# First stage of a four-stage block: channels on the partitions from the scan to the output projection

## What is computed

```python
def _mamba_block(x, in_proj_w, conv_w, conv_b, dt_bias, A_log, D, norm_w, out_proj_w, ln_w, ln_b):
    zxbcdt = jnp.einsum('bld,ed->ble', x, in_proj_w)
    z = zxbcdt[..., :D_INNER]
    ...
    def step(h, inp):
        dA_t, x_t, B_t, C_t, dt_t = inp
        dBx = dt_t[:, :, None, None] * x_t[..., None] * B_t[:, None, None, :]
        h = h * dA_t[:, :, None, None] + dBx
        y = jnp.einsum('bhpn,bn->bhp', h, C_t)
        return (h, y)
    ...
    y = ys.transpose(1, 0, 2, 3) + D[None, None, :, None] * x_ssm
    y = y.reshape(b, l, D_INNER)
    y = y * jax.nn.silu(z)
    y = y * lax.rsqrt(jnp.mean(y * y, axis=-1, keepdims=True) + EPS) * norm_w
    y = jnp.einsum('bld,ed->ble', y, out_proj_w) + x
    mu = jnp.mean(y, axis=-1, keepdims=True)
    var = jnp.mean((y - mu) ** 2, axis=-1, keepdims=True)
    return (y - mu) * lax.rsqrt(var + EPS) * ln_w + ln_b
```

## Time and profile before

| | |
|---|---|
| median of 3 runs | 1599.17 us (1599.06 to 1600.42) |
| profiled execution | 1601.12 us, span of its instructions 1599.2 us |
| TensorE busy | 1442.7 us, 90% of the span |
| VectorE busy | 1209.4 us, 76% |
| ScalarE busy | 820.1 us, 51% |
| GpSimd busy | 796.9 us, 50% |
| granted TensorE clock | 0.969 of full speed, on average |
| first three layers | to about 1080 us |
| last layer | from there to the end |

### The profile page before, as it was taken

One profiled execution on the slowest core, in us unless ns is written; L12 is line 12 of the kernel. 1 busy time (PEld: TensorE's weight loads), 2 busy tenths in 40 slices (PEclk: granted clock), 3 DMA queues, 4 the chain that ended last, 5 costly groups with the idle time before them and its releaser, 6 DMA issues. The chain is left out here.

```text
span 1599.2 us, 32323 instructions
## 1 busy us (share of the span) xinstructions
PE 1442.7 (90%) x10752; PEld 1262.2 (79%) x10752; DVE 1209.4 (76%) x2290; ACT 820.1 (51%) x1846; POOL 796.9 (50%) x2004
## 2 busy tenths in 40 slices
PE   5588999999999999999999999754999999869997
PEld 4366788788888788887888877543999999869997
DVE  4466798898898898898898887533888888827664
ACT  2234544544544545545445443202676777557775
POOL 0332253563563463463563552233777777657763
PEclk9997999999999999999999999866999999989999
DMA  6000000000000000000000000006677766867782
GB/s 233 7 7 1 8 1 14 15 1 14 15 1 14 14 2 14 15 1 14 15 1 14 8 5 5 7 7 207 177 197 197 191 184 191 265 245 302 302 323 70
DMA packets 140752, 132.10 MB, mean 83 GB/s; under 512 B 7376, under 2 KB 130512, under 8 KB 134096
## 3 DMA queue, kind: packets, MB, share of 16 engines
q1 hardware_dynamic: 140624, 130.50, 25.9%
HBM read 73.85 MB, written 56.62 MB: 82 GB/s over the span
## 5 line engine op out<-in xcount | busy, mean ns | idle before, releaser
L622 PE MATMUL bk<-ve_f,oe 128*128 128x128 f32 x2048 | 277.0, 279 | 2.6 <-DVE ve_f L1300 2.6
L622 PEld LDWEIGHTS bk<-ve_f,oe 128*128 128x128 f32 x2048 | 249.7, 192 | 25.9 <-issue 20.7
L1300 DVE SCALAR_TENSOR_TENSOR ve_f<-ps_m,oT 128x512 f32<-128x512 f32 x256 | 171.8, 679 | 5.2 <-PE bk L622 3.4
L2187 POOL TENSOR_TENSOR d_s<-d_ex 128x1024 f32<-128x1024 f32 x32 | 131.8, 4120 | 87.1 <-ACT d_ex L1987 87.1
L1261 DVE COPY_PREDICATED vals<-oh,bk 128x1024 f32<-128x1024 int32 x112 | 146.6, 1309 | 10.6 <-PE bk L393 8.8
L1937 PE MATMUL d_sl<-d_ex,e_prT 128*128 128x128 f32 x1024 | 135.8, 276 | 9.4 <-POOL d_ex L2204 9.4
L1871 PE MATMUL d_lg<-d_phf,d_xtf 128*128 (+1 forms) x1024 | 125.0, 282 | 15.9 <-DMA d_xtf<-x_T 6.8
L1871 PEld LDWEIGHTS d_lg<-d_phf,d_xtf 128*128 128x128 f32 x1024 | 122.0, 199 | 16.8 <-issue 7.1
L1937 PEld LDWEIGHTS d_sl<-d_ex,e_prT 128*128 128x128 f32 x1024 | 125.2, 193 | 9.7 <-POOL d_ex L2204 9.7
L1881 PE MATMUL d_sl<-d_ex,d_xs 128*128 128x128 f32 x1024 | 121.4, 277 | 5.7 <-DVE d_ex L2102 5.7
L1881 PEld LDWEIGHTS d_sl<-d_ex,d_xs 128*128 128x128 f32 x1024 | 118.5, 194 | 6.1 <-DVE d_ex L2102 6.1
(11 more groups left out here) (283 smaller groups left out, 3733.4 us busy)
## 6 DMA issues: line engine op xcount, KB each, us to landing
logits<-d_raw SPq DMA_DIRECT2D x128, 256.0 KB, 3.3
e_lt<-logits SPq DMA_DIRECT2D x32, 1024.0 KB, 5.6
y_slots<-d_ys SPq DMA_DIRECT2D x64, 256.0 KB, 4.3
d_ex<-y_slots SPq DMA_DIRECT2D x16, 1024.0 KB, 7.3
d_w<-W SPq DMA_DIRECT2D x16, 256.0 KB, 3.4
oe<-xT SPq DMA_DIRECT2D x1, 2048.0 KB, 7.8
xt_in<-xT SPq DMA_DIRECT2D x16, 128.0 KB, 2.3
x_in<-x SPq DMA_DIRECT2D x16, 128.0 KB, 2.4
```

The source lines that it names most:

```text
L622: last = pe.matmul(ps_u[:, cols], oe[:, hp, e, :], mo[:, n % MO, hp, :], start=False, stop=(e == NE - 1 and hp == HP - 1), skip_group_chec ...
L1300: V.scalar_tensor_tensor(mo[:, n % MO, :, :].rearrange("p a n -> p (a n)"), ps_m[:], float(NE - e), oT[:, u, c, :, :].rearrange("p a n -> ...
L2187: G.tensor_tensor(s8[:], part[:, 0:8, :], part[:, 8:16, :], ALU.add).then_inc(n, 1)
```

## The change

From the scan to the output projection, all tiles of stage a now have channels on the partitions.

- `a_z` swaps its operands: `sz` and `tz` are 2 groups of channels x 256 tokens.
- VectorE's `a_xd` makes only `xd`.
- The running sum leaves `a_bg`. In `a_state` it is now made per channel and token: four products, two for each group of channels, each with a column of `a_all` repeated 64 times as weights and `upp_s` streamed. `ep` is 128x256, made by ScalarE after it has copied `st`.
- `a_inter` is two products of 128 columns instead of one of 256.
- VectorE's `a_int` is a product with `ep` into the right half of `inter`, and two operations that add D times `xbc` (two groups).
- `a_y` swaps its operands: 64 columns of `xd` are the weights and the 128 columns of `mx` are streamed; the two heads of a group end in the two halves of the partitions.
- ScalarE squares `yg` in one operation without accumulator. The sums are made on TensorE, in a new step `a_ssq` between `b_values(6)` and the next sequence's `a_xbc`: four products with 128 columns of `sq` as weights and one column of ones. ScalarE copies the two columns to `ssq`, between `c_gelu` and `a_cin`.
- The transposes `a_yt` and the copy to `yT` are gone. `a_op` reads `yg` and stands where `a_yt` stood.
- `a_xt` stays. Temporaries of the preparation now share the place of `lx`, and two constants are filled before the first slot.

```diff
@@ TensorE @@
             def a_bg(b):
 
-                wait(pe, q["a_xd"], 2 * b + 2)
+                wait(pe, q["a_xd"], b + 1)
                 pe.transpose(ps_a[:, 0:P], xbc[:, 2, 0:P], id_f[:])
...
-                pe.matmul(ps_a[:, 3 * P:3 * P + NH], upp_s[:], a_all[:, b * C + 1, :], start=True, stop=True,
-                          skip_group_check=True).then_inc(q["a_bg_ps"], 1)
...
             def a_state(b):
                 wait(pe, q["a_gm"], b + 1)
-                wait(pe, q["a_ep"], b + 1)
                 wait(pe, q["a_btok"], b + 1)
                 wait(pe, q["a_xst"], b + 1)
                 pe.matmul(ps_a[:, 0:DI], btok[:], xst[:].rearrange("p h d -> p (h d)"),
-                          start=True, stop=True, skip_group_check=True).then_inc(q["a_st_ps"], 1)
+                          start=True, stop=True, skip_group_check=True)
+                for j in range(2):
+                    for a in range(2):
+                        half = slice(64 * a, 64 * a + 64)
+                        head = 2 * j + a
+                        last = pe.matmul(ps_a[half, DI + j * P:DI + (j + 1) * P],
+                                         a_all[:, b * C + 1, head:head + 1].to_broadcast([P, HD]), upp_s[:],
+                                         start=True, stop=True, skip_group_check=True)
+                last.then_inc(q["a_st_ps"], 1)
...
             def a_y(b):
                 wait(pe, q["a_mx"], C * b + C)
-                wait(pe, q["a_int"], 2 * b + 1)
+                wait(pe, q["a_int"], 3 * b + 1)
+                for j in range(2):
+                    for c in range(C):
+                        for a in range(2):
+                            half = slice(64 * a, 64 * a + 64)
+                            last = pe.matmul(ps_a[half, j * L + c * P:j * L + (c + 1) * P], xd[:, c, 2 * j + a, :],
+                                             mx[:, c, 2 * j + a, :], start=True, stop=True, skip_group_check=True)
+                last.then_inc(q["a_y_ps"], 1)
+
+            def a_ssq(b):
+
+                wait(pe, q["a_sq"], b + 1)
+                wait(pe, q["b_eg"], b)
+                wait(pe, q["b_x2t"], b - 2)
                 for c in range(C):
-                    for h in range(NH):
-                        last = pe.matmul(ps_a[:, c * DI + h * HD:c * DI + (h + 1) * HD], mx[:, c, h, :],
-                                         xd[:, c, h, :], start=True, stop=True, skip_group_check=True)
-                last.then_inc(q["a_y_ps"], 1)
-
-            def a_yt(b, more):
+                    for j in range(2):
+                        last = pe.matmul(ps_o[:, c:c + 1], sq[:, j, c * P:(c + 1) * P], ones[:],
+                                         start=(j == 0), stop=(j == 1), skip_group_check=True)
+                last.then_inc(q["a_ssq_ps"], 1)
+
+            def a_op(b, more):
                 wait(pe, q["a_yg"], b + 1)
                 if more:
                     wait(pe, q["a_cin"], 2 * b + 4)
...
@@ ScalarE @@
             def a_sq(b):
 
                 wait(act, q["a_yg"], b + 1)
-                for c in range(C):
-                    if c == 1:
-                        wait(act, q["a_sq"], C * b + 1)
-                    nc.scalar.activation(sq[:], yg[:, c, :], ACT.Square, scale=0.5, accum_out=ssq[:, c:c + 1]
-                                         ).then_inc(q["a_sq"], 1)
-
-            def a_yt(b):
-                wait(act, q["a_yt_ps"], b + 1)
-                wait(act, q["a_op_ps"], b)
-                copy(yT[:].rearrange("p j n -> p (j n)"), ps_a[:]).then_inc(q["a_yt"], 1)
+                wait(act, q["a_ssq_ps"], b)
+                nc.scalar.activation(sq[:], yg[:], ACT.Square, scale=0.5).then_inc(q["a_sq"], 1)
+
+            def a_ssq(b):
+                wait(act, q["a_ssq_ps"], b + 1)
+                wait(act, norms["rms"]["rstd"], RSQRT_OPS * b)
+                copy(ssq[:], ps_o[:, 0:C]).then_inc(q["a_ssq"], 1)
@@ VectorE @@
                 V.tensor_tensor(xd[:], ps, dt_all[:, b * C:(b + 1) * C, :].unsqueeze(3).to_broadcast([P, C, NH, HD]), ALU.mult
                                 ).then_inc(q["a_xd"], 1)
-                V.tensor_tensor(xD[:], ps, d_h[:].unsqueeze(1).unsqueeze(3).to_broadcast([P, C, NH, HD]), ALU.mult
-                                ).then_inc(q["a_xd"], 1)
...
-                V.tensor_tensor(inter[:], ps_a[:, DI:2 * DI].rearrange("p (h d) -> p h d", h=NH),
-                                ep[:].unsqueeze(2).to_broadcast([P, NH, HD]), ALU.mult).then_inc(q["a_int"], 1)
-                wait(dve, q["a_int"], 2 * b + 1)
-                V.tensor_tensor(xD[:, 1, :, :], xD[:, 1, :, :], inter[:], ALU.add).then_inc(q["a_int"], 1)
+                V.tensor_tensor(inter[:, :, P:L], ps_a[:, 0:DI].rearrange("p (j t) -> p j t", j=2), ep[:], ALU.mult
+                                ).then_inc(q["a_int"], 1)
+                wait(dve, q["a_int"], 3 * b + 1)
+                for j in range(2):
+                    V.scalar_tensor_tensor(xD[:, j, :], xbc[:, j, :], d_h[:, j:j + 1], inter[:, j, :], ALU.mult, ALU.add
+                                           ).then_inc(q["a_int"], 1)
```

More of the change, by code:

```diff
@@ L272, in token_blocks @@
         names = """a_xbc_ps a_cin a_conv a_th a_xbc a_z_ps a_tz a_sz a_am a_seg_ps a_lx a_mx a_xt_ps a_xd
-            a_bg_ps a_btok a_ep a_gm a_xst a_st_ps a_st a_int_ps a_int a_y_ps a_y a_yg a_sq a_yt_ps a_yt
+            a_bg_ps a_btok a_ep a_gm a_xst a_st_ps a_st a_int_ps a_int a_y_ps a_y a_yg a_sq a_ssq_ps a_ssq
             a_op_ps a_r a_xb a_n a_x1t_ps a_x1h a_x1l a_x1
@@ L472, in a_yt @@
                     wait(pe, q["a_cin"], 2 * b + 4)
[L473 to L480 removed]
                 for c in range(C):
                     for j in range(2):
[L483 removed]
+                        last = pe.matmul(ps_a[:, c * D:(c + 1) * D], yg[:, j, c * P:(c + 1) * P], out_w[:, j, :],
                                          start=(j == 0), stop=(j == 1), skip_group_check=True)
@@ L534, in b_oht @@
                 wait(pe, q["b_x2t"], b - 1)
+                wait(pe, q["a_ssq"], min(b + 2, NB))
                 pe.transpose(ps_o[:, P:2 * P], oh[:].rearrange("p c h e -> p (c h e)"), id_f[:]
@@ L747, in slot @@
                     b_values(t - 1, 1 - u, 6)
+                if a:
+                    a_ssq(t)
                 if more:
@@ L764, in slot @@
                 if a:
-                    a_yt(t, more)
+                    a_op(t, more)
                 if b:
@@ L773, in slot @@
                     c_kv(t - 3)
-                if a:
-                    a_op(t)
                 if b:
@@ L910, in a_btok @@
                 copy(btok[:], ps_a[:, 0:P]).then_inc(q["a_btok"], 1)
-                wait(act, q["a_int"], 2 * b)
-                nc.scalar.activation(ep[:], ps_a[:, 3 * P:3 * P + NH], ACT.Exp).then_inc(q["a_ep"], 1)
             def a_st(b):
```

87 lines of the change are left out of this document (41 added, 46 removed).

## The result

| | before | after |
|---|---|---|
| median of 12 runs each, side by side | 1600.82 us | 1605.83 us |
| lowest, highest | 1598.27, 1602.51 | 1602.30, 1611.04 |
| profiled execution, its span | 1601.12, 1599.2 | 1611.04, 1609.1 |
| median length of a full slot | 59.04 us | 59.37 us |

What follows compares the result with a forecast made beforehand. A slot was bound by a TensorE stretch to the last value product, then VectorE and ScalarE to `rgS`. Added 0.9 us less 0.75 slack gave 0.15 us in 14 slots: 1599.17 + 2.1 = 1601.3 us, range 1595.5 to 1609.

Steps and rivals of the forecast that it cites:

- main case: Whole kernel: a full slot grows by 0 to 0.3 us, giving 1599 to 1604 us; chance 0.45.
- VectorE is late at the squares: Rival at `a_ssq`: `yg` slips a further 0.4 us, TensorE waits, the period grows 0.55, 1607 us; chance 0.25.
- TensorE ahead of the last value product: Step summing TensorE's changes in `a_bg`, `a_state`, `a_inter`, `a_y` and `a_ssq`: +0.9 us a slot.
- sign (1): Expected in TensorE's profile: `a_y` 1.1 us to the next line, the four `a_state` products 0.7, `a_ssq` 0.9.
- VectorE: Step on VectorE's work: dropping the product with D gains nothing, `a_int` +0.2 us, squares ready within 0.1 us of `a_ssq`.
- `ra` 0.15 us later: VectorE reaches `ra` at 642.08 - 0.75 + 0.9 = 642.23, so `ra` starts 0.15 us later than before.
- eats the slack first: Work added to TensorE ahead of 633.22 first uses 0.75 us of slack at `ra`, then is paid in full.
- `c_out` also moves by some 0.15. From there the slot is as before: TensorE's `c_out` waits for `kv`, ending at 642.31, and moves by some 0.15 us; nothing behind it changes further.
- One-column products: Rival at `a_ssq`: a one-column pass costs much less than 0.11 us, giving 1595 us; chance 0.17.
- The halves side by side: Passes into two halves overlap in `a_y` and `a_state`; the rival, no overlap, gave 1612 us, chance 0.07.
- The last layer and the first slots: Last layer takes what it took; effects in the first two slots about cancel, leaving 14 slots that grow.
- six signs: `a_y`, `a_state`, `a_ssq` times; `kv` wait replaces `kr`; no projection wait; longer value-product wait; `rgS` wait stays; slots 59.2 us.

Runs made afterwards that it cites:

- e3: Kernel before plus four unread one-column products on TensorE behind value product 6, where `a_ssq` stands in the changed kernel: ratio 1.0077, slots of 59.97 us.
- e10: Changed kernel with `a_op` back behind `c_kv` and a 128x512 ScalarE copy where the one to `yT` was: ratio 1.0100, slots of 60.07 us.
- e8: Changed kernel with TensorE's second turning of probabilities (three transposes) moved ahead of `c_out`: ratio 1.0022 to the kernel before, slots of 59.18 us.
- e2: Changed kernel with the sums of squares in one pass each instead of two, from squares rounded to F32R: ratio 1.0008, slots of 59.00 us.
- e4: Kernel before plus four unread one-column products on TensorE ahead of `b_rgb(2)`, where it waits for `rgS`: ratio 1.0004, slots of 59.03 us.
- e6: Changed kernel with `a_y`'s products ordered all of the first 64 weight columns, then all of the second, not alternating: ratio 1.0060, slots of 59.77 us.

## Why the prediction was right, and where its sizes were off

The sign and the range were right, and so was the main cause: the time is slower, by a slot that grew because TensorE has more to do ahead of the last value product, and on the scale of the forecast it is 1599.2 + 5.0 = 1604.2 us, inside 1595.5 to 1609. The size was too small, 2.1 for 5.0 us, and the slot's 0.33 lies just above the 0 to 0.3 that I gave the main case. That the range held it is in part luck: its upper side was there for VectorE being late at the squares, which didn't happen, and not for `c_out`. By its steps:

- *TensorE ahead of the last value product:* +0.9 forecast, +0.99 in the slot shown. I measure each step from the last value product ahead of it to the second pass behind it, so that its borders count. `a_state` cost +0.77 for 0.68 (its four new products took 0.59 up to the next line, where sign (1) said 0.7, but L446 ahead of them 0.52 where it took 0.25), and `a_y` gave -0.52 for -0.6. With 0.11 us for a pair of passes side by side, going into the halves and out again cost 0.33 and 0.31 us: the 0.24 that I had taken from `b_pv` was too small. `a_ssq` cost +0.97 for 0.89, of which 0.88 are its own and 0.09 fall on L400 behind it (0.76 us to the next line for 0.67). `a_bg` gave -0.34 for -0.15, with part of a wait for VectorE that went too; `a_inter` cost 0.02 for 0.1. That is 0.90, and 0.09 more are spread over the value products between.
- *VectorE:* `a_int` took 1.24 us, +0.17 for +0.2, and the squares came just in time, as forecast. The rival "VectorE is late at the squares" didn't happen.
- *`ra` 0.15 us later:* +0.16. The number was right, though reached by a false sentence, which is luck. I subtracted 0.75 us of slack as if it were the loop's. It was VectorE's alone (e3), so "eats the slack first" doesn't hold for the kernel before. The changed kernel could use it because the copy to `yT` and the place of `a_op` had gone, worth 0.70 us a slot (e10); without these the slot would have been 1.03 longer.
- *"`c_out` also moves by some 0.15. From there the slot is as before":* this is the step that failed. `kv` came as forecast (+0.92). `c_out` started 0.24 later, since TensorE took up the first product 0.05 after `kv` ended, and this product had its weights still to load: the load starts with it at 648.53, where in before it starts 0.11 us ahead of it. So its two passes take 0.33 us to the next line, 0.22 in before (642.14 to 642.36). That makes +0.34 at the scores of the second pair, the same at the third's, and VectorE's `b_max` of the third pair waits 0.11 us for these. So TensorE's path, not `ra`, set the slot, and e8 shows it: with the wait filled, slots of 59.18, very near the forecast's 59.2.
- *One-column products:* 0.11 a pass (8 in 0.88 us), as I had taken, so that rival is out. The Trainium skill's rule ("TensorEngine Tiling (Array Packing)", Instruction Overhead) would have made it 0.2 us in all, an estimate from the page; here the measurement decides. A pass with 128 columns of weights took 0.11 us with 1, 2 (e2's four in 0.45), 64 and 128 streamed columns alike, which fits a bound by the loading of the weights.
- *The halves side by side:* yes, 1.07 us for `a_y`, so that rival is out too.
- *The last layer and the first slots:* 14 x 0.33 is 4.6 of 5.0 us. The last layer took 506.3 us in the profiled execution for 504.2, and 503.1 to 504.9 in the profiled executions of all ten variants built on the changed kernel, so it is the execution, not the change. Whether the rest is in the first slots can't be told: the second and third took 107.6 to 110.8 us together in the three traces with the kernel before's order (before, e3, e4), and 109.4 to 115.0 in the others.

All six signs of the list were seen, except two sizes: the four products of `a_state` in (1), and in (6) the slots, 59.37 us apart, not 59.2.

## What to carry to other kernels

Slack read at one wait is that engine's alone: before adding work ahead of it, follow what the engine is waiting for, and ask if that hangs on the same work. Once a wait is removed, several paths lie within a tenth of a microsecond, so carry the shift along each of them to the next point where they meet, with the loading of weights that a wait uncovers. And look at the duration of small operations, not only at the waits: one that takes two or three times its usual length can itself be a wait.

## What I had not expected of the hardware

- VectorE's product with two inputs in SBUF, started under a GpSimd product, ends 17 to 22 ns after it (113 of 113 that start more than 6 ns ahead of its end), lengthened from 0.16 to as much as 0.53 us.
- Passes into the two halves of the partitions run side by side where they are within a few passes of each other in the queue, alternating or not: 0.055 us apart in the middle of e6's `a_y`, 0.11 at its ends.
- Going into the halves and out again cost TensorE 0.31 to 0.33 us beyond the passes, in `a_y` and `a_state`.
- A product of 128 columns that follows a wait takes 0.33 us to the next line for its two passes, and 0.22 in a stream.
